# Q, K and V from three products of fp32r high and low parts, with the norm's weight folded into the weights, in a four-stage transformer kernel

## What is computed

```python
zn = (z - mu) / jnp.sqrt(var + 1e-05) * ln_w + ln_b
qkv = (zn @ W_qkv + b_qkv).reshape(b, n, 3, H, DH)
...
scores = jnp.einsum('bhqd,bhkd->bhqk', q, k) * scale
attn = jax.nn.softmax(scores, axis=-1)
msa = jnp.einsum('bhqk,bhkd->bhqd', attn, v)
```

## Time and profile before

| | us |
|---|---|
| median of 3 executions | 1663.95 (1661.17 to 1665.4) |
| the profiled execution, its own time | 1662.2 |
| its span, first to last instruction | 1660.4 |
| PE busy | 1520.8 (92%) |
| DVE busy | 1294.4 (78%) |
| ACT busy | 918.6 (55%) |
| POOL busy | 291.9 (18%) |
| mean granted TensorE clock | 0.966 of full |

### The profile page before, as it was taken

One profiled execution on the slowest core, in us unless ns is written; L12 is line 12 of the kernel. 1 busy time (PEld: TensorE's weight loads), 2 busy tenths in 40 slices (PEclk: granted clock), 3 DMA queues, 4 the chain that ended last, 5 costly groups with the idle time before them and its releaser, 6 DMA issues.

```text
span 1660.4 us, 28734 instructions
## 1 busy us (share of the span) xinstructions
PE 1520.8 (92%) x10902; PEld 962.5 (58%) x10902; DVE 1294.4 (78%) x2481; ACT 918.6 (55%) x1398; POOL 291.9 (18%) x383
## 2 busy tenths in 40 slices
PE   5977999999299999799999979999998999999886
PEld 2747899999153334785433368643336764333675
DVE  3585566543369998897999989799997979999596
ACT  1212344444137887344788834568884355888532
POOL 0063233220411120301112021111110310000030
PEclk9988999999599999899999999999999999999998
DMA  4125878776233220003421000232200022220000
GB/s 141 52 77 168 257 247 256 247 249 200 90 58 75 53 43 8 1 1 67 90 53 43 8 1 1 64 79 52 53 15 1 1 49 54 40 40 3 1 1 26
DMA packets 80308, 123.10 MB, mean 74 GB/s; under 512 B 13657, under 2 KB 55898, under 8 KB 80170
## 3 DMA queue, kind: packets, MB, share of 16 engines
q1 hardware_dynamic: 70794, 93.46, 21.5%
q0 software_dynamic: 9376, 27.80, 5.7%
HBM read 76.84 MB, written 18.61 MB: 57 GB/s over the span
## 4 chain that ended last, share of the span: by engine, by line
PE 74%; DVE 16%; ACT 5%; issue 3%; DMA 1%; POOL 1%; SPq 0%; DVEq 0%; ACTq 0%; POOLq 0%
PE PS L1096 15%; PE PS L1049 13%; PE PS L973 8%; PE PS L961 7%; PE PS L1082 6%; DVE MX L1630 6%; PE PS L1205 4%; PE PS L1215 4%; PE PS L1019 3%; PE PS L1033 2%; PE PS L911 2%; PE PS L1166 2%; PE PS L1239 1%; DVE OT L1484 1%; PE PS L950 1%
## 5 line engine op out<-in xcount | busy, mean ns | idle before, releaser
L1630 DVE TENSOR_REDUCE MX<-PS 128x1 f32<-128x512 f32 x1024 | 635.1, 684 | 29.5 <-PE PS L1049 25.4
L763 ACT ACTIVATE Pb<-PS 128x1024 f32<-128x1024 f32 x512 | 519.3, 1025 | 122.5 <-PE PS L1082 119.4
L1049 PE MATMUL PS<-Ks,Qs 48*128 48x512 f32 x1024 | 386.5, 454 | 1.6 <-DVE MX L1630 0.9
L1082 PE MATMUL PS<-Qs,Ks 50*128 50x512 f32 x1024 | 360.5, 451 | 0.0
L1096 PE MATMUL PS<-Pb,V 128*32 128x256 f32 x4096 | 320.5, 390 | 0.5
L1049 PEld LDWEIGHTS PS<-Ks,Qs 48*128 48x128 f32 x1024 | 160.1, 184 | 203.8 <-DVE MX L1630 138.1
L1096 PEld LDWEIGHTS PS<-Pb,V 128*32 128x32 f32 x4096 | 83.9, 108 | 164.3 <-ACT Pb L763 109.7
L1082 PEld LDWEIGHTS PS<-Qs,Ks 50*128 50x128 f32 x1024 | 143.9, 185 | 24.0 <-ACT Pb L763 19.8
L973 PE MATMUL PS<-Pb,OT 128*128 128x256 f32 x624 | 141.0, 379 | 0.0
L961 PE MATMUL PS<-Ks,Qs 128*128 128x256 f32 x936 | 127.4, 294 | 6.3 <-DVE Ks L1506 4.8
L961 PEld LDWEIGHTS PS<-Ks,Qs 128*128 128x128 f32 x936 | 119.6, 196 | 8.7 <-DVE Ks L1506 5.8
(11 more groups left out here) (296 smaller groups left out, 2105.7 us busy)
## 6 DMA issues: line engine op xcount, KB each, us to landing
Pb<-W SPq DMA_DIRECT2D x78, 512.0 KB
y_slot<-V SPq DMA_DIRECT2D x39, 256.0 KB
Qs<-Qh SPq DMA_DIRECT2D x128, 64.0 KB, 2.3
Ks<-Kh SPq DMA_DIRECT2D x120, 64.0 KB, 2.3
V<-b SPq DMA_DIRECT2D x39, 128.0 KB
XT<-x_mid POOLq DMA_DIRECT2D x4, 1024.0 KB, 6.6
out<-Pb POOLq DMA_DIRECT2D x4, 1024.0 KB, 6.7
OT<-xT SPq DMA_DIRECT2D x2, 1024.0 KB, 6.5
```

Of the source, the lines that this page charges most:

```text
L763: F["ex"].inc(act.activation(weights_of(n), PS[:, 2 * (n % 2):2 * (n % 2) + 2, :], ACT.Exp, scale=0.25))
L1049: F["slp"].inc(pe.matmul(PS[:, slot_bank(i), :], Qs[rows, p % NB, t * P:(t + 1) * P], Ks[rows, p % NB, kh * HALF:(kh + 1) * HALF], start=T ...
L1082: ins = pe.matmul(PS[:, 2 * (n % 2) + a, :], Ks[rows, p % NB, kt * P:(kt + 1) * P], Qs[rows, p % NB, qh * HALF:(qh + 1) * HALF], start=Tru ...
L1630: F["sld"].inc(dve.tensor_reduce(MX[:, p % 2, a, t, kh:kh + 1], PS[:, slot_bank(i), :], AX.X, ALU.max))
```

## The change

- `qk_unit` and `values` use three fp32r products for each fp32 one: high weights x high tokens, low weights x high tokens, high weights x low tokens. That is six matmuls per unit in place of two fp32 ones (four records).
- `turned` is a plain copy into XTH, the high part. A new DVE step, `x_halves`, takes PSUM minus XTH into XTL, four times 128x512 per sequence. PE's units wait for all four (`xtl`). XTH and XTL lie in Ks[:, 2:4] and Qs[:, 2:4].
- The norm's weight is multiplied into `wqkv` by DVE (`ws`), its bias goes through the weights by 12 one-column matmuls on PE (`wb`) into `bqkv`, and `wqkv` is split into `wqH` (ACT) and `wqL` (DVE): all once, between the last expert tile and the first sequence.
- `wqkv` has no tile of its own: it is loaded into V's space after expert tile 10's weights are issued, on SP.
- Slots 2 and 3 of Ks are overwritten by XTH each sequence. So SP writes their rows of ones in each sequence (4 DMAs), after `maxima_row(0)` and after all eight V units, ahead of stacks 2 and 3; PE waits for these rows at pair 2. Before the first sequence ones go to slots 0 and 1 only.
- At the joint, unit 0 stands behind the transposes of tile 7, and unit 1 behind down 7. ACT takes out tile 7's transposes before unit 0, and DVE does `x_halves` directly behind the last rounding.

```diff
-            load(wqkv[:, :, :], Wqkv.rearrange("(c p) n -> p c n", p=P), s_late)
...
+                if k == 10:
+                    sp.dma_start(wqkv, Wqkv.rearrange("(c p) n -> p c n", p=P)).then_inc(s_wqkv, 16)
...
                 maxima_row(0)
+                F["vp"].wait(sp, b, TT)
+                for k in range(2, NB):
+                    one_rows(k, F["onr"])
                 for p in range(2, NB):
...
-                    F["xt"].inc(act.activation(XT[:, c, th * HALF:(th + 1) * HALF], PS[:, u, :], ACT.Identity,
-                                               scale=lnw[:, c:c + 1], bias=lnb[:, c:c + 1]))
+                    F["xt"].inc(act.activation(XTH[:, c, th * HALF:(th + 1) * HALF], PS[:, u, :], ACT.Copy))
...
+            C["ws"].wait(act, DC)
+            C["qh"].inc(act.activation(wqH[:, :, :], wqkv, ACT.Copy))
...
+            for j in range(3 * DC):
+                for kc in range(DC):
+                    ins = pe.matmul(PS[:, 1, j:j + 1], wqkv[:, kc, j * P:(j + 1) * P], lnb[:, kc:kc + 1],
+                                    start=(kc == 0), stop=(kc == DC - 1))
...
                 for kc in range(DC):
...
-                    ins = pe.matmul(o, wqkv[:, kc, w * D + c * P:w * D + (c + 1) * P], tokens,
-                                    start=(kc == 0), stop=(kc == DC - 1))
+                    for q, (weight, x) in enumerate(((wqH, XTH), (wqL, XTH), (wqH, XTL))):
...
+                        ins = pe.matmul(o, weight[:, kc, w * D + c * P:w * D + (c + 1) * P], tokens,
+                                        start=(kc == 0 and q == 0), stop=(kc == DC - 1 and q == 2))
...
+            def x_halves(b, ahead):
...
+                    F["xtl"].inc(dve.tensor_tensor(XTL[:, c, at], PS[:, u, :], XTH[:, c, at].bitcast(F32), ALU.subtract))
...
+            C["wb"].wait(dve, 1)
+            pro(dve.tensor_tensor(bqkv[:, :], PS[:, 1, 0:3 * DC], bqkv[:, :], ALU.add))
+            for kc in range(DC):
+                C["ws"].inc(dve.tensor_scalar(wqkv[:, kc, :], wqkv[:, kc, :], lnw[:, kc:kc + 1], None, ALU.mult))
+            C["qh"].wait(dve, 1)
+            C["ql"].inc(dve.tensor_tensor(wqL[:, :, :], wqkv, wqH[:, :, :].bitcast(F32), ALU.subtract))
```

More of the change, by code:

```diff
@@ L104, in transformer @@
         lnb = sb("lnb", [P, DC])
-        wqkv = sb("wqkv", [P, DC, 3 * D])
+        wqH = sb("wqH", [P, DC, 3 * D], F32R)
+        wqL = sb("wqL", [P, DC, 3 * D], F32R)
         bqkv = sb("bqkv", [P, 3 * DC])
@@ L184, in transformer @@
         MR = sb("MR", [2 * TT, 2, P], F32R)
-        ones = sb("ones", [2, S])
+        ones = sb("ones", [2, QW])
         rc = sb("rc", [P, 2, HEADS])
@@ L192, in transformer @@
         R2 = Vf[:, 0:TT * D].rearrange("p (t d) -> p t d", t=TT)
+        wqkv = Vf[:, 4 * S - DC * 3 * D:4 * S].rearrange("p (c n) -> p c n", c=DC)
         Pbf = Pb[:, :, :, :].rearrange("p k g n -> p (k g n)")
@@ L234, in transformer @@
         XFh, XFl = Qs[:, 0:2, :], Qs[:, 2:4, :]
+        XTH, XTL = Ks[:, 2:4, :], Qs[:, 2:4, :]
         SGb, Hb, qn_h, qm_h, HQ = (OTf[:, k * I:(k + 1) * I] for k in range(5))
@@ L258, in transformer @@
         s_late = sem("s_late")
+        s_wqkv = sem("s_wqkv")
         s_wqn = sem("s_wqn")
@@ L440, in _, with one_rows @@
             sp.wait_ge(s_one, 1)
-            for k in range(NB):
+            def one_rows(k, done):
                 for a in range(2):
-                    sp.dma_start(Ks[ROW * a + STACK:ROW * a + MROWS, k, :].bitcast(F32), ones[:, :]).then_inc(s_one, 16)
+                    done.inc(sp.dma_start(Ks[ROW * a + STACK:ROW * a + MROWS, k, :].rearrange("o (r n) -> o r n", n=QW).bitcast(F32),
+                                          ones[:, :].unsqueeze(1).to_broadcast([2, S // QW, QW])), by=16)
+            for k in range(2):
+                one_rows(k, C["one"])
             for b in range(B):
@@ L611, in _ @@
             sequence(B - 1, False)
-            pool.wait_ge(s_one, 1 + 16 * 2 * NB)
+            C["one"].wait(pool, 16 * 2 * 2)
         @block.scalar
@@ L916, in warm @@
                 for _ in range(n):
-                    ins = pe.matmul(PS[:, bank, :], ident[:, :], wqkv[:, 0, 0:HALF], start=True, stop=True)
+                    ins = pe.matmul(PS[:, bank, :], ident[:, :], wproj[:, :, :].rearrange("p c n -> p (c n)"), start=True, stop=True)
             def ranks(g):
@@ L993, in _ @@
             second_layer(TILES - 1)
-            pe.wait_ge(s_one, 1 + 16 * 2 * NB)
+            pe.wait_ge(s_wev, len(turns))
+            pe.wait_ge(s_wlo, len(low_turns))
+            pe.wait_ge(s_wqkv, 16)
+            for j in range(3 * DC):
+                for kc in range(DC):
+                    ins = pe.matmul(PS[:, 1, j:j + 1], wqkv[:, kc, j * P:(j + 1) * P], lnb[:, kc:kc + 1],
+                                    start=(kc == 0), stop=(kc == DC - 1))
+            C["wb"].inc(ins)
+            C["one"].wait(pe, 16 * 2 * 2)
             def turn(b, ahead):
@@ L1032, in values @@
                     for kc in range(DC):
-                        ins = pe.matmul(PS[:, value_bank(t), 0:D], XT[:, kc, t * P:(t + 1) * P], wqkv[:, kc, 2 * D:3 * D],
-                                        start=(kc == 0), stop=(kc == DC - 1))
+                        for q, (weight, x) in enumerate(((wqH, XTH), (wqL, XTH), (wqH, XTL))):
+                            ins = pe.matmul(PS[:, value_bank(t), 0:D], x[:, kc, t * P:(t + 1) * P], weight[:, kc, 2 * D:3 * D],
+                                            start=(kc == 0 and q == 0), stop=(kc == DC - 1 and q == 2))
                     F["vp"].inc(ins)
@@ L1077, in transposed_scores @@
                         F[f"mrow{qh}"].wait(pe, b, 16 * 2 * (p + 1))
+                    if n == 2 * KT * 2:
+                        F["onr"].wait(pe, b, 16 * 4)
                     if n >= 2:
@@ L1230, in sequence @@
                         down(t - 1)
-                    if more and t == TT - 1:
-                        F["xt"].wait(pe, b, 4, 1)
-                        qk_unit(b, 1, 0)
                     F["hq"].wait(pe, b, t + 1)
@@ L1243, in sequence @@
                 if more:
-                    qk_unit(b, 1, 1)
+                    F["xtl"].wait(pe, b, 4, 1)
+                    qk_unit(b, 1, 0)
                 down(TT - 1)
                 if more:
-                    for u in (2, 3):
+                    for u in (1, 2, 3):
                         qk_unit(b, 1, u)
             turn(0, 0)
-            F["xt"].wait(pe, 0, 4)
+            C["ql"].wait(pe, 1)
+            F["xtl"].wait(pe, 0, 4)
             for u in range(4):
@@ L1577, in ahead_norm @@
                                                      rstd[:, :, :], ALU.mult, ALU.mult))
+            def x_halves(b, ahead):
+                for u in range(4):
+                    c, th = u // 2, u % 2
+                    F["xt"].wait(dve, b, u + 1, ahead)
+                    at = slice(th * HALF, (th + 1) * HALF)
+                    F["xtl"].inc(dve.tensor_tensor(XTL[:, c, at], PS[:, u, :], XTH[:, c, at].bitcast(F32), ALU.subtract))
             def qk_low(b, ahead, units):
@@ L1757, in sequence @@
                         ahead_norm(b, 1, step)
+                if more:
+                    x_halves(b, 1)
                 ffn_add(TT - 2)
@@ L1777, in _ @@
                 F["xw"].inc(dve.tensor_scalar(XN[:, t, :], R[:, t, :], rstd[:, 0, t:t + 1], nmr[:, 0, t:t + 1], ALU.mult, ALU.add))
+            x_halves(0, 0)
             qk_low(0, 0, range(4))
```

27 lines of the change are left out of this document (13 added, 14 removed), and 2 rows, old and new, of the table C.

## The result

The changed kernel took 1672.85 us (median of 20 executions, 1662.37 to 1682.28) against 1662.54 for the kernel before (20 executions, 1659.75 to 1665.6) on the same chip: a ratio of 1.0057, 95% interval 1.0041 to 1.0073. It is slower by some 10 us; the forecast was 1653.8, faster. The spread is a result too: 20 us between executions of one program, where the kernel before has 6.

A forecast was written before the change was run, and what follows sets the result against it. Bound: PE behind the feed-forward's last rounding, then DVE's maxima. Joints 7.5 plus sequence 0's 3.1, less 0.2 for gathers and 0.2 for the wqkv load, make 10.2 us less: 1653.8 us from the median, range 1649.5 to 1660.0.

The forecast's parts named there:

- the clock falls at the joints: Rival: PE's new idle times at the joints bring half-clock stretches, two in each of three joints giving 1672 us; chance 0.06.
- Each new idle time is followed by dense work: Argument against a clock fall at the joints: dense PE work follows each new wait, 4 us behind the first.
- the price of 3.0 us: Cost of one half-clock stretch on PE, 6.86 - 3.83 us, read from two groups of gate/up.
- Unit: Q and K units on PE: six products cost 1.35 us (bounds 1.32 and 1.39), 0.40 less than now.
- x_halves: New DVE step at the joint: four end 2.5 us after the last rounding, when unit 0 starts.
- The stack, not PE, is late: At the joint pair 0's stack copies hold the first score tile; the first maximum gains 1.7 us.
- 17 maxima without a gap: Behind the first maximum at a joint: DVE-bound, 10.25 us; the 18th comes 2.5 us earlier per joint.
- SP's four ones: Four extra DMA issues on SP per sequence, 2.5 us, fit its idle time ahead of the second maxima row: 0.
- The wqkv load: Load moved into the expert stage behind tile 10: costs 0.2 us, bounds 0 and 4.9.
- The rival with a chance of 0.08: The wqkv load stalls an expert tile as the dear feed-forward load did: 1658.5 us; chance 0.08.
- Before sequence 0: Units ahead of the first sequence get cheaper, partly at half clock; the 18th maximum gains 3.1 us.
- The gathers: POOL's gathers before sequence 0, slowed by new DVE work beside them: 0.2 us lost.

The follow-up runs named there:

- e1: The changed kernel once more, unaltered, in its own group of executions: 1673.18 us, ratio 1.0079.
- e9: The kernel before, with SP issuing five copies of pair 1's stack ahead of pair 0's three Ks copies at the three joints: 1667.22 us, ratio 1.0026.
- e4: The changed kernel with the load of wqkv issued behind the last expert tile's loads in place of tile 10's: 1672.25 us, ratio 1.0063.
- e2: The changed kernel with six useless products ahead of unit 0's wait and six ahead of the first score tile: 1662.8 us, ratio 1.0000.
- e13: The changed kernel, unit 1 ahead of down 7, V 0 ahead of the scores, wqkv loaded late, six useless products ahead of unit 0 at joints: 1654.17 us.
- e6: The changed kernel with six useless products ahead of unit 0's wait only, none ahead of the first score tile: 1679.52 us, ratio 1.0104.
- e7: The changed kernel with V from one fp32 product of the high parts, its low parts left out: 1683.47 us, ratio 1.0114.
- e10: The changed kernel with unit 1 ahead of down 7 and V 0 ahead of the first score tiles: 1659.99 us, ratio 0.9996.
- e8: The changed kernel, useless products ahead of unit 0 and the first score tile, wqkv loaded late, 22 useless products before sequence 0's transposes: 1669.01 us.
- e12: e13 with useless products before sequence 0 too: six ahead of unit 0, 31 behind the fifth gathered tile, one behind each of six transposes: 1652.85 us.

## Why the prediction was wrong

**The step that failed is the rival "the clock falls at the joints".** It named three idle times and their lengths (1.6, 1.5 and 1.6 us). The trace has 1.5 ahead of unit 0 and 1.6 (2.0 at joint 1) ahead of the first score tile; ahead of the turn of maxima it has only 0.5. The forecast gave the fall a chance of 0.06 and put its cost at nothing, and two things in that were wrong. "Each new idle time is followed by dense work" was no protection: e1 and e9 ran 17.1 and 26.8 us busy at half clock. And the price of 3.0 us was read from a stretch of gate/up. Behind the first score tile the stretch lasts 13.7 to 27.3 us and costs 6 to 11 (37.2, 39.1 and 40.0 us against 31.4 to 31.8, and 44.6 against 34.0, at undisturbed joints). One of them in an execution eats most of the forecast's gain. That the rival's time, 1672, is the one measured is luck: it came from six stretches of 3.0 us, and half of the miss has other causes, below. I had the mechanism and its places, and argued its chance away by a reason that no row supported. What the trace did show, six half-clock stretches of 3.4 to 6.8 us in the four feed-forwards of the kernel before (two, one, two and one, where the prediction counted one each), should have weighed more.

**The terms of the sum.** Where the clock held, they were off as follows.

- *Unit:* 1.40 us, as six products stand 0.233 us apart (1.35 forecast; the upper bound, 1.39, was just passed). It did not matter; the stack held TensorE.
- *x_halves:* 2.48 us forecast as 2.5; unit 0 ran from 2.5 us behind the rounding on. Right.
- *The stack, not PE, is late:* right. SP's first copy went 10.1 us behind the rounding (9.95 forecast), the last 15.1 (14.95). It landed 3.35 us later, not 2.4 to 2.7: the earlier trace rows is a median over 28 copies and says nothing of this one. Why it is slower no run tells. The same copy took 3.4 and 3.8 us at joints 2 and 1, and before sequence 0 it took 3.2 us here and 2.4 in e1. Together 0.96 us at the first maximum: a gain of 0.75, not 1.7.
- *17 maxima without a gap:* right, 10.47 us [0.65 ahead of them, none inside]. But V took 0.90 us a unit and not 0.72. Six products of 256 columns between score tiles cost 0.2 us that the row of 24 alike ones does not contain. V ended at 1379.9, not by 1374, and behind it stand ACT's copy of V and two products (L1129), so the turn came at 1380.88. POOL's split had been done since 1380.35 (timeline below). DVE idled 1.75 us where it had idled 1.91. That is the other 0.5 us of the joint: 31.4 in place of 29.9.
- *SP's four ones:* free, as forecast. The second row of maxima was issued 1393.87 - 1381.42 = 12.45 us behind the first (12.5 forecast).
- *The wqkv load:* 2 to 5 us, forecast 0.2 with a bound of 4.9. The rival with a chance of 0.08 came true. I had put it with the cheap load of the two in the earlier trace rows by the shape of its rows, which was no guide. e4 shows that the stall leaves with the load.
- *Before sequence 0:* x_halves and the waits left a gain of 0.8 us from the last gather to the 18th maximum (43.1 in place of 43.9), not 3.1. The clock rose 5.7 us behind unit 0's start. The forecast took the 3.8 us of the trace before: at its own half-clock price two units need 5.4 us, and it had them done in 4.35. And the first score tile waited 1.8 us for its stack.
- *The gathers:* 21.0 us in place of 19.9, 1.1 lost, forecast 0.2.

POOL's split of the first maxima in the changed kernel; it answers the earlier trace rows:

```profile
1380.15 0.20 POOL L564 TENSOR_TENSOR NMs<-NM,NMs 128x8 fp32r<-128x8 f32 x1
```

Timelines of the changed kernel before sequence 0, DVE's wqL step and POOL's gathers; they answer:

```profile
426.73 1.76 DVE L1807 TENSOR_TENSOR wqL<-V,wqH 128x1536 fp32r<-128x1536 f32 x1 [1.55 <-ACT wqH L858]
```
```profile
426.18 1.00 POOL L536 DMA_INDIRECT Qh<-y_slot,posb  x1 [0.16 <-issue]
427.49 1.83 POOL L536 DMA_INDIRECT Kh<-y_slot,posb  x1 [0.31 <-issue]
429.62 0.95 POOL L536 DMA_INDIRECT Qh<-y_slot,posb  x1 [0.30 <-issue]
```

The gather whose first 1.00 us lies beside the subtraction took 1.83 us, 0.88 more than the one behind it. The gather ahead of it has 0.45 us beside the subtraction and took 1.00, as it did in the kernel before. The prediction had cited the Trainium skill (GPSIMD Engine Reference, "1. Specifications") for contention beside an operation with two SBUF inputs; the 1.83 us agree with it in direction. It is one gather that pays, not the 3.4 us that I had set as the rule's price; two later ones took 1.18 and 1.12 us beside DVE's combining, where one of the kernel before took 1.13.

**The balance.** From -10.2 to +10.3 us are 20.5 us. By the first profile the joints' own terms are 3 x 1.5 = 4.5, the later end of the experts 3.0 (2.0 of it the load's stall, the rest not traced), the gathers 1, sequence 0's units 2.3: 10.8. That the other 10 are the clock is an estimate: by the prices above, one long stretch and one or two short ones in a typical execution. Filling the waits (e2) gives back 10. Removing the stack's wait with useful work, loading wqkv late and filling unit 0's wait (e13) gives 19.

**What stays open** is why a long stretch came in 3 of 12 executions of e9 and, judged by time and clock, in most of the changed kernel's, at nearly the same wait. The idle time ahead of unit 0, 16 us before the stack's wait, is not what is missing in e9, since e6 has it filled and all four of its executions are slow. The cheap V units are not it (e7). The cheap products of the Q and K units, x_halves, and that DVE and not TensorE sets the pace behind the wait, were not tested with that wait. Nor is it known what in the work behind a wait makes the stretch short or long. For the load: e4 shows that at tile 10 it stalls a tile, and behind the last tile there is none left to stall, so these runs do not separate its place from its size or the shape of its rows.

## What to carry to other kernels

When a change makes TensorE's work cheaper, look first for the waits that it uncovers: here 0.35 us per unit was saved, and a wait of 1.6 us for a DMA that used to be hidden cost more than the joints gained. Price a new idle time of TensorE by what the clock may do behind it (here up to 27 us at half clock), and judge such a kernel by many executions: the first profile alone had caught a good one. Take the wait away with work that is needed (a unit moved ahead, so that the copies start sooner; an independent product in front of the wait), as e10 did, and put filler only into what is left.

## What the runs showed of the hardware that was not expected

- A wait of 1.6 us, in a kernel that is otherwise full, can be followed by 27.3 us of nearly unbroken work at half clock (e9). Which joint it hits differs between executions, and in the changed kernel, on one core, the time at half clock goes with the spread of 20 us (correlation 0.96).
- Two idle times of the same length, 1.5 and 1.6 us, are followed by stretches of quite different lengths, 3.4 us behind the one ahead of unit 0 and 13.7 to 27.3 behind the one ahead of the first score tile. The work behind them differs, but that this is the reason was not tested.
- Among short transposes 0.5 us apart a clock just gained fell again (e8, 4.03 us busy of 6.70). With a product in six of the gaps, and more filler ahead of and behind the transposes, it was kept (e12, 5.88 of 6.50).
- The last of nine SBUF to SBUF copies of 64 KB issued 0.63 us apart landed 3.35 to 3.8 us behind its issue at the three joints of the changed kernel; the median of such copies in the kernel before was 2.4.
